# A cross-attention block with a gated expert layer on one core: key parts stored once, a beginning ordered by need, and the maxima moved by GpSimd's DMA queue

## The reference

```
q = layernorm(x) @ wq.T + bq          # [16, 256, 128]
k = ctx @ wk.T + bk ; v = ctx @ wv.T + bv   # [16, 1601, 128]
attn = softmax(q k^T / sqrt(8)) v     # for each of 16 heads
x = x + tanh(g_xattn) * (attn @ wd.T + bd)
h = layernorm(x)
gate = top 2 of 8 experts of sigmoid(h @ gate_W) * route_scale, normalised
x = x + tanh(g_ffn) * (sum_e gate_e * expert_e(h) + shared(h))   # gelu MLPs, hidden 64
```

## Time and profile before

| | |
|---|---|
| median of 3 runs | 1434.74 us (1431.17 to 1438.01) |
| the profiled execution | 1436.73 us, span of its profile 1434.9 us |
| busy | TensorE 1241.7, ScalarE 1055.6, VectorE 1049.3, GpSimd 418.7 us |
| DMA | 147.13 MB, 47.4% of 16 engines' span |
| stages | start to 111 us, middle to 1337 us, tail to 1435 us |

### The profile page before, as it was taken

The page is one execution under the profiler, slowest core; times in us unless marked ns, Lnnn a source line. Parts: engine busy times, 40 slices in busy tenths (PEclk is TensorE's granted clock), DMA queues, the critical chain, the costliest instruction groups (busy, mean ns, idle before and its releaser), DMA issues.

```text
span 1434.9 us, 29778 instructions
## 1 busy us (share of the span) xinstructions
PE 1241.7 (87%) x11555; PEld 458.9 (32%) x11555; DVE 1049.3 (73%) x1208; ACT 1055.6 (74%) x1962; POOL 418.7 (29%) x309
## 2 busy tenths in 40 slices
PE   2448889798989999899989999799979999799855
PEld 1112323232323433243323333243323433243224
DVE  8477778587768888688868878688768868689001
ACT  1008879587978799688968789688968889689741
POOL 7242224051333215151424125051423205010111
PEclk6568999798988999899989999899989999899786
DMA  7673634636273653737273744637173744501101
GB/s 213 114 149 69 150 70 98 140 84 129 53 164 70 139 119 87 147 81 149 52 169 61 170 87 99 139 82 146 47 167 67 165 92 96 102 11 33 31 14 45
DMA packets 71390, 147.13 MB, mean 103 GB/s; under 512 B 13705, under 2 KB 37970, under 8 KB 71250
## 3 DMA queue, kind: packets, MB, share of 16 engines
q1 hardware_dynamic: 71250, 145.24, 47.4%
HBM read 88.30 MB, written 56.91 MB: 101 GB/s over the span
## 4 chain that ended last, share of the span: by engine, by line
PE 66%; DMA 14%; ACT 5%; DVE 4%; SPq 4%; POOL 3%; issue 2%; POOLq 0%; ACTq 0%; DVEq 0%
PE o_ps L775 26%; PE a_ps L757 15%; PE b_ps L741 11%; DMA m_dram<-nm_parts 10%; PE a_ps L688 4%; PE a_ps L692 4%; ACT probs L573 3%; PE b_ps L720 2%; DVE run_max L901 2%; SPq L406 2%; DMA q_op<-m_dram 1%; SPq L397 1%; PE a_ps L684 1%; PE b_ps L723 1%; DMA q_op<-q_dram 1%
## 5 line engine op out<-in xcount | busy, mean ns | idle before, releaser
L901 DVE TENSOR_REDUCE run_max<-b_ps 128x2 f32<-128x1024 f32 x768 | 899.4, 1218 | 249.4 <-PE b_ps L741 246.0
L573 ACT ACTIVATE probs<-a_ps 128x512 f32<-128x512 f32 (+1 forms) x1664 | 901.9, 594 | 144.3 <-PE a_ps L757 127.4
L775 PE MATMUL o_ps<-probs,v_op 128*32 128x256 f32 (+3 forms) x4928 | 505.8, 483 | 2.3 <-ACT probs L573 1.2
L757 PE MATMUL a_ps<-q_op,k_op 51*128 51x256 bf16 (+1 forms) x3328 | 338.1, 283 | 46.4 <-DMA q_op<-m_dram 25.6
L741 PE MATMUL b_ps<-k_op,q_op 48*128 48x512 bf16 (+1 forms) x2048 | 325.6, 350 | 37.5 <-DVE run_max L901 24.2
L757 PEld LDWEIGHTS a_ps<-q_op,k_op 51*128 51x128 bf16 (+1 forms) x3328 | 112.9, 97 | 373.5 <-ACT probs L573 307.3
L741 PEld LDWEIGHTS b_ps<-k_op,q_op 48*128 48x128 bf16 x2048 | 88.7, 96 | 208.2 <-DVE run_max L901 95.9
L775 PEld LDWEIGHTS o_ps<-probs,v_op 128*32 128x32 f32 (+1 forms) x4928 | 98.4, 109 | 176.4 <-issue 93.8
L509 POOL TENSOR_TENSOR attn<-num,den_all 128x256 f32<-128x256 f32 x16 | 11.6, 728 | 440.3 <-DMA den_all<-r_dram 440.3
L688 PE MATMUL a_ps<-kctx,wk_s 128*128 128x400 f32 (+1 forms) x128 | 81.4, 734 | 55.7 <-DMA kctx<-ctx_t 49.9
L469 POOL TENSOR_TENSOR nm_parts<-nm_t,one 8x256 bf16<-8x256 f32 x32 | 19.3, 602 | 360.5 <-ACT nm_t L605 360.5
(11 more groups left out here) (100 smaller groups left out, 680.4 us busy)
## 6 DMA issues: line engine op xcount, KB each, us to landing
k_op<-k_dram SPq DMA_DIRECT2D x64, 600.4 KB, 9.5
k_dram<-k_parts SPq DMA_DIRECT2D x32, 600.4 KB, 6.0
kctx<-ctx_t SPq DMA_DIRECT2D x16, 800.5 KB, 12.5
vctx<-ctx_t SPq DMA_DIRECT2D x16, 800.5 KB, 11.8
k_dram<-k_parts SPq DMA_DIRECT2D x32, 400.2 KB, 7.0
o_dram<-o_s SPq DMA_DIRECT2D x32, 256.0 KB, 2.1
g_all<-g_dram SPq DMA_DIRECT2D x16, 512.0 KB, 6.4
k_dram<-k_parts SPq DMA_DIRECT2D x32, 200.1 KB, 6.7
```

The source lines that it names most:

```text
L573: act.activation(probs[0:keys, unit % PB, :], a_ps[at % AB][0:keys, :], ACT.Exp, scale=SCALE).then_inc(a_taken, 1)
L757: last = pe.matmul(a_ps[(at + side) % AB][0:KEYS[t], SEQ * a:SEQ * a + SEQ], k_op[buf][rows, slot, 128 * t:128 * t + KEYS[t]], q_op[buf][r ...
L775: last = pe.matmul(o_ps[32 * j:32 * j + 32, cols], v_op[s // 2 % 2][0:KEYS[t], t, GP * (s % 2) + j, :], probs[0:KEYS[t], unit % PB, cols], ...
L901: dve.tensor_reduce(run_max[:, t, :, p, c:c + 1].rearrange("q v o -> q (v o)"), slot[:, :, :], AX.X, ALU.max).then_inc(b_taken, 1)
```

## The change

Four edits. `k_dram` holds the three parts once; a store is two DMAs, and a load of keys is three DMAs a side, of 24, 16 and 8 rows (with the two for queries, eight a step instead of four). `move_maxima` goes from SyncE's program to GpSimd's, right behind `split_maxima`. The load of `kctx` for batch b+3 goes from odd steps to even steps, behind `load_operands`, `spread_sums` and `spread_gates`. And the beginning is ordered anew: tokens are loaded in three pieces where they are needed, the first `vctx` comes after the operands of steps 0 and 1, ScalarE issues the query stores of chunk 0, and `first_maxima` orders step -2 as five row-score units, the other work, five row-score units, and step -1 as its 16 row-score units of step 0, T, and then the rest.

```diff
-OP_DMAS = 4
+OP_DMAS = 2 * (len(PLACES) + 1)
-PART_STORES = 2 * len(PLACES)
+PART_STORES = 2
+def first_maxima():
+    scores = [event for event in ORDER[-2] if event[0] == "S"]
+    rest = [event for event in ORDER[-2] if event[0] != "S"]
+    first = [event for event in ORDER[-1] if event[0] == "S" and event[1] < SUNITS]
+    turn = [("A", ("T", 0, 0))]
+    return scores[:5] + rest + scores[5:], first + turn + [e for e in ORDER[-1] if e not in first + turn]
+
+ORDER[-2], ORDER[-1] = first_maxima()
...
-        k_dram = nc.dram_tensor("k_dram", [2, 2, len(KPART), 64, CTX], BF16, kind="Internal").ap()
+        k_dram = nc.dram_tensor("k_dram", [2, 2, 3, 64, CTX], BF16, kind="Internal").ap()
...
-            sp.dma_start(x_s[:, 0:4, :], x[:, 0:4, :]).then_inc(x0_in, 16)
+            def load_tokens(c0, c1, arrived):
+                for c in range(c0, c1):
+                    sp.dma_start(x_s[:, 4 * c:4 * c + 4, :], x[:, 4 * c:4 * c + 4, :]).then_inc(arrived, 16)
+            load_tokens(0, 1, x_in[0])
...
-            for c in range(1, CHUNKS):
-                sp.dma_start(x_s[:, 4 * c:4 * c + 4, :], x[:, 4 * c:4 * c + 4, :]).then_inc(x_in, 16)
...
-                    sp.dma_start(k_op[buf][rows, :, :].rearrange("r (a p) c -> r a p c", a=2),
-                                 kd[:, :, pairs, :]).then_inc(op_in[buf], 16)
+                    for r0, r1 in PLACES:
+                        to = slice(SIDE * side + DH * r0, SIDE * side + DH * r1)
+                        sp.dma_start(k_op[buf][to, :, :].rearrange("r (a p) c -> r a p c", a=2),
+                                     kd[0:DH * (r1 - r0), :, pairs, :]).then_inc(op_in[buf], 16)
...
                 for a in range(2):
-                    for r0, r1 in PLACES:
-                        sp.dma_start(k_dram[b % 2, a, r0:r1].rearrange("n r c -> r n c"),
-                                     k_parts[64 * a:64 * a + 64, 0:r1 - r0, :]).then_inc(k_written, 16)
+                    sp.dma_start(k_dram[b % 2, a].rearrange("n r c -> r n c"),
+                                 k_parts[64 * a:64 * a + 64, :, :]).then_inc(k_written, 16)
...
+            store_keys(0)
+            load_operands(0)
+            load_context("K", kctx, 1, kctx_in)
+            load_tokens(1, 2, x_in[1])
+            load_operands(1)
             load(vctx, ctx_t[0]).then_inc(vctx_in, 16)
-            store_keys(0)
-            load_context("K", kctx, 1, kctx_in)
-            store_queries(0)
-            load_operands(0)
+            load_tokens(2, CHUNKS, x_in[2])
             for s in range(FIRST, LAST + 1):
...
-                if 0 <= s + 3 < STEPS:
+                if s % 2 == 0 and 2 <= s + 3 < STEPS:
                     load_operands(s + 3)
...
-                if s % 2 == 1 and b + 3 < BATCH:
+                if s % 2 == 1 and 2 <= s + 3 < STEPS:
+                    load_operands(s + 3)
+                if s % 2 == 0 and b + 3 < BATCH:
                     load_context("K", kctx, b + 3, kctx_in)
...
-                if 0 <= s + 1 < STEPS:
-                    move_maxima(s + 1)
...
+            def move_maxima(s):            # now in GpSimd's program
+                h = s % 2
+                pool.wait_ge(m_chain, 4 * (s + 1))
+                if s >= 2:
+                    pool.wait_ge(m_in[h], 32 * (s // 2))
+                pool.dma_start(m_dram[h].rearrange("n h q -> h n q"), nm_parts[:, :, :]).then_inc(m_written, 16)
+                pool.wait_ge(m_written, 16 * (s + 1))
+                for side in range(2):
+                    pool.dma_start(q_op[s % 4][SIDE * side + ROWS:SIDE * side + MROWS, :, :],
+                                 m_dram[h, :, GP * side:GP * side + GP, :]).then_inc(m_in[h], 16)
...
                     split_maxima(s + 1)
+                    move_maxima(s + 1)
...
                 aux_unit(*unit)
+            store_queries(act, 0)
...
-                dve.wait_ge(x_in, 16 * (CHUNKS - 1))
...
+                            if s < 4:
+                                dve.wait_ge(x_in[s // 4 + 2], 16 if s < 0 else 16 * (CHUNKS - 2))
                             statistics("q", (s + 6) // 4)
```

More of the change, by code:

```diff
@@ L264, in flamingo_block @@
         y_s = sb("y_s", [128, 4, 128])
-        key_in, first_in, const_in, x0_in, x_in, ones_set = (sem(n) for n in ("key_in", "first_in", "const_in", "x0_in",
-                                                                              "x_in", "ones_set"))
+        key_in, first_in, const_in, ones_set = (sem(n) for n in ("key_in", "first_in", "const_in", "ones_set"))
+        x_in = [sem(f"x_in{i}") for i in range(3)]
         k_ones, v_ones = [sem(f"k_ones{i}") for i in range(4)], sem("v_ones")
@@ L297, in keys_split, with store_queries @@
                 engine.wait_ge(k_chain, 4 * b)
+        def store_queries(engine, c):
+            engine.wait_ge(q_chain, 4 * (c + 1))
+            for a in range(2):
+                for part, (r0, r1) in enumerate(PLACES):
+                    for r in range(r0, r1):
+                        engine.dma_start(q_dram[2 * c:2 * c + 2, a, r].rearrange("b r q -> r b q"),
+                                         q_parts[64 * a:64 * a + 64, part, :]
+                                         .rearrange("p (b q) -> p b q", b=2)).then_inc(q_written, 16)
         block = ctx.enter_context(nc.Block())
@@ L395, in store_keys @@
                 for a in range(2):
-                    for r0, r1 in PLACES:
-                        sp.dma_start(k_dram[b % 2, a, r0:r1].rearrange("n r c -> r n c"),
-                                     k_parts[64 * a:64 * a + 64, 0:r1 - r0, :]).then_inc(k_written, 16)
-            def store_queries(c):
-                sp.wait_ge(q_chain, 4 * (c + 1))
-                for a in range(2):
-                    for part, (r0, r1) in enumerate(PLACES):
-                        for r in range(r0, r1):
-                            sp.dma_start(q_dram[2 * c:2 * c + 2, a, r].rearrange("b r q -> r b q"),
-                                         q_parts[64 * a:64 * a + 64, part, :]
-                                         .rearrange("p (b q) -> p b q", b=2)).then_inc(q_written, 16)
-            def move_maxima(s):
-                h = s % 2
-                sp.wait_ge(m_chain, 4 * (s + 1))
-                if s >= 2:
-                    sp.wait_ge(m_in[h], 32 * (s // 2))
-                sp.dma_start(m_dram[h].rearrange("n h q -> h n q"), nm_parts[:, :, :]).then_inc(m_written, 16)
-                sp.wait_ge(m_written, 16 * (s + 1))
-                for side in range(2):
-                    sp.dma_start(q_op[s % 4][SIDE * side + ROWS:SIDE * side + MROWS, :, :],
-                                 m_dram[h, :, GP * side:GP * side + GP, :]).then_inc(m_in[h], 16)
+                    sp.dma_start(k_dram[b % 2, a].rearrange("n r c -> r n c"),
[5 more added lines that the diff above has]
+            load_operands(1)
             load(vctx, ctx_t[0]).then_inc(vctx_in, 16)
-            store_keys(0)
-            load_context("K", kctx, 1, kctx_in)
-            store_queries(0)
-            load_operands(0)
+            load_tokens(2, CHUNKS, x_in[2])
             for s in range(FIRST, LAST + 1):
@@ L934, in _ @@
             dve.memset(k_op[0][:, :, :], 1.0).then_inc(k_ones[0], 1)
-            dve.wait_ge(x0_in, 16)
+            dve.wait_ge(x_in[0], 16)
             statistics("q", 0)
```

2 lines of the change are left out of this document (1 added, 1 removed).

## The result

| | before | after |
|---|---|---|
| median | 1432.95 us (4 runs beside it) | 1470.81 us (1464.12 to 1482.87) |
| ratio, 95% interval | 1 | 1.0276 [1.0196, 1.0356] |
| profiled execution | 1436.73 us | 1464.12 us, span 1462.3 us |

A forecast was written before the change was run, and what follows sets the result against it. TensorE was taken as the bound. Stalls -60.8, half-clock time -59, left-over stalls +15, more waiting for ScalarE and VectorE +8, start -4: together -101 from the median of 1434.7, so 1334 us, range 1303 to 1396.

The forecast's parts named there:

- The path taken as 7 us: Last split to maxima in `q_op` through GpSimd: 7 us against 6 available, leaving 1 us at 15 turns, 15 us.
- a queue of its own: Maxima's store at the turn: slow (12.6 against 1.4 us) from what lies ahead in SyncE's queue; GpSimd's queue avoids that.
- Rival E: Store of the maxima or context held by something else, DMA bandwidth, not order: 1425 to 1440 us; chance 0.04.
- rival A: GpSimd's path takes 9 us, a stall of 3 at each turn (45 us): -31, 1404 us; chance 0.11.
- rival B: GpSimd's path over 10.1 us loses; at 12 us, stalls of 6 and half clock, +53, 1488 us; chance 0.06.
- Some 5 us there cost nothing: Key and query splits behind GpSimd's wait for its store: key parts are stored later, queries read a step later; no cost.
- Three issues in software: GpSimd's issuing of the maxima's store and loads: with some sharing of DMA engines, the quiet 3.4 us is doubled.
- `kctx` earlier: -36.7 us of waits: Context load issued up to a step (about 40 us) ahead: TensorE's 36.7 us wait in the middle goes.
- Three parts: I count 0: Key stores halved, about 6 us of DMA time per batch saved; TensorE waits for neither stores nor loads: 0.
- rival D: Loads in 24, 16, 8 rows: operands 12.5 us instead of 9.4, middle nothing, start +2, 1340 us; share 0.3 of forecast's 0.70.
- The start: -4 forecast: Before the first score pair: step 0's operands 11 us sooner, late `vctx` 0 leaves a gain of 4 us.
- The size of the prize: Whole kernel: stalls -60.8, half-clock time -59, with the other terms together -101, giving 1334 us.

The follow-up runs named there:

- a2: Kernel before with one edit, the maxima moved by GpSimd instead of SyncE: 1479.4 us, 1.032 of the kernel before.
- c1: Kernel before, SyncE's order alone changed: maxima ahead of odd steps' operand loads and vctx, kctx load behind the maxima in even steps: 1387.1 us, 0.970.
- b1: Changed kernel, with SyncE's query stores behind the output moves of the next step instead of ahead of them: 1470.3 us, 1.028 of the kernel before.
- g2: c3 with GpSimd issuing the maxima's store and loads, SyncE waiting at the same place until they are down: 1434.0 us, 0.997 of the kernel before.
- e1: Kernel before, six parts kept, only the loads of keys cut into pieces of 24, 16 and 8 rows: 1538.3 us, 1.072.
- e2: Kernel before, six parts kept, only the loads of keys cut into three pieces of 16 rows: 1462.1 us, 1.019.
- a4: Kernel before with only the new start, `first_maxima` and the order of loads ahead of the loop: 1440.4 us, 1.004.
- h2: f1 with the kctx load in even steps, and it and the vctx load behind the maxima's moves: 1338.4 us, 0.934 of the kernel before.
- a3: Kernel before with one edit, three key parts in memory, loaded in 24, 16 and 8 rows: 1421.1 us, 0.990.
- f1: Kernel before with three key parts in memory, ordered 1, 0, 2, so loads are three pieces of 16 rows: 1364.7 us, 0.950.
- c3: c1 with the vctx load and query stores also moved behind the output moves of the next even step: 1367.0 us, 0.952 of the kernel before.

## Why the prediction was wrong

**"The path taken as 7 us", "a queue of its own": the step that failed.** It read 12.6 against 1.4 us for the same 12 KB and put the difference down to order in the queue. Rival E had the right cause ("DMA bandwidth, not order") and was set aside by those same two numbers, which do not tell the two apart. On its own queue the store takes 10.8 us at that turn (a2); on the old queue, ahead of the loads, 1.7 (c1). The Trainium skill, page "DMA: Bandwidth & Descriptors", section "Queues, rings and completion order", says that each DMA engine takes turns between the queues at the granularity of a packet; no run here shows the turns, and whatever they give, it is not enough. So the path is 10.9 us and not 7 before steps divisible by 4, while 6.7 before the other even steps is what was taken, and 40.3 us were spent on the maxima where the sum had 15. By size that is rival A (45 us, chance 0.11); rival B's path of over 10.1 us stands only at every second turn. What the profile shows beyond A no rival had: the wait for VectorE, 38.3 us in place of 7.9, a clock of 0.94 as before, where the sum and A both had half-clock time gone, and a start 9 us longer. a2 alone costs 3.2%, some 45 us.

**"Some 5 us there cost nothing" failed too.** The sentence stopped at the queries being read a step later. On SyncE the output moves stand behind the query stores, and they lead to VectorE and TensorE within 17 us. By a2's waits this step is no smaller than the first: 16.6 us more for VectorE, 9.7 more for the maxima. But b1 takes the wait for VectorE away and the loss reappears elsewhere, so how much of the 45 us is the longer path and how much the late splits is not told apart. g2, where SyncE waits at the maxima's place and the query stores are out of the way, still loses 67 us.

**"Three issues in software": about right.** The store's issue takes 0.63 us and that of the two loads 1.04, against 0.27 and 0.56 on SyncE, and a quiet store, its issue included, 2.2 against 1.4 us: 1.3 us more in all. The estimated 4 to 5 us for a chain of two fits the shortest path that TensorE waited for, 4.9 us. It is the loaded turns that it leaves out.

**`kctx` earlier: -36.7 us of waits.** Right in the waits, wrong in the time: alone it gives 0.3%, since the wait for the maxima, still behind the loads on SyncE, takes its place.

**"Three parts: I count 0" failed, twice over.** Some 6 us of DMA time per batch were seen to go, and were called worthless because TensorE does not wait for stores. But the stores share the DMA engines with all that TensorE does wait for: halved, they are worth 7 to 8%, 97 us with even pieces and 117 with uneven ones. That is 6 to 7 us for each of 16 batches, near the 6 us seen to go, though no run shows that the two are the same time. Against it stands rival D: mechanism right, start price somewhat low (12.5 us and 2.4 to land forecast, 17.2 to 17.7 measured), "in the middle nothing" wrong: of the 93 us that uneven pieces add to the profiled execution, 82 lie between the first score pair and the last. The two nearly cancel (0.990), so the 0 was close by luck. By the rule that D named (the Trainium skill, page "DMA: Bandwidth & Descriptors", section "Why a DMA increments its semaphore by 16 and not by 1"), 24, 16 and 8 rows spread over 12, 16 and 8 engines; the DMA share of 0.78 and 0.85 in e1 against 1.07 and 1.03 in e2 agrees.

**The start: -4 forecast, +9 measured in the profile, +0.4% alone.** The queries were taken as stored at 31.6 and the operands as landed at 43.4; they were asked for at 34.56 and needed 17.7 us. Everything behind came later in turn, `vctx` by 17 us. With whole loads (a4) the new order still brings the first score pair at 114.3 us, 3.5 later than before.

**The size of the prize was right.** Removing both waits and the half clock was priced at -101 us, with four steps in 149 us, a clock of 0.98 or more and 1334 us. h2 removes them with three parts and SyncE's order alone: 150.8 us, 0.98 and 1338 us. Part of that nearness is luck: by the profiles h2's middle is 75 us shorter, where the sum had 97 without the start, and its start is 14 us shorter, where it had 4; and VectorE's waits are not those of the sum. The prediction knew roughly what was to be had and not what the change would do about it.

**Open.** Whether halved stores gain by their bytes (2.4 to 1.2 MB a batch) or by their DMAs (six to two) was not separated. Nor was what else differs in both pairs (a3 and e1, f1 and e2): with three parts in memory the loads read two of the parts more than once, from the same place, where with six each piece is read from its own. How much of g2's 67 us comes from SyncE's longer hold rather than from GpSimd's path was not measured either.

## What to carry to other kernels

In this kernel a small transfer was late because of the bytes in flight when it was issued; ask what the DMA engines are carrying at that moment, and issue it ahead of them, rather than give it another queue. A transfer that no engine waits for is not free, since it slows those that are waited for; so cut its bytes, and keep the pieces of a load equal. But measure it in the order at hand: three parts with equal pieces gave 5% in the old order and cost 2% in c3's. Before a wait is put on an engine, follow what is queued behind it through every queue to the engine that sets the time.

## What the runs showed of the hardware

- The same 12 KB store: 12.6 us behind loads in its queue, 10.8 us on another queue beside them (means over eight such moves 12.4 and 10.1), 1.4 us at a quiet place, 1.7 us issued ahead of them.
- Cutting a load of 48 rows in three cost 1.9% with 16, 16, 16 rows and 7.2% with 24, 16, 8, for the same bytes.
- Issuing that store holds GpSimd for 0.63 to 0.70 us (once 0.84) and SyncE for 0.27 to 0.33, and at a quiet place it took 2.2 against 1.4 us.
- Halving the stores of the keys, which no engine waits for, was worth 7 to 8% of the kernel.
